# Weighing values with the values held still in TensorE and the probabilities streaming, in a local-and-global attention kernel

## The reference

```
x = x + attn(layernorm(x));  out = x + layernorm(x) @ (weight * scale[:, None]).T + bias
attn:  q, k, v = h @ Wq + bq, h @ Wk + bk, h @ Wv + bv      (split into 16 heads of 64)
  local:  each block of 128 queries sees 256 keys, from 64 before the block to 64 behind it
          ctx = softmax(q k^T / 8, outside the sequence masked) v
  global: the 62 queries with the largest norm, the first and the last see all 1024 keys;
          their rows of ctx are replaced by softmax(qg k^T / 8) v
```

## Time and profile before

| | us |
|---|---|
| median of 3 runs | 2242.92 (2241.53 to 2243.91) |
| the profiled execution's own time | 2242.39 |
| its span from first to last instruction | 2240.8 |
| TensorE busy in the span | 2166.2 (97%) |
| VectorE busy | 1486.8 (66%) |
| ScalarE busy | 827.8 (37%) |
| GpSimd busy | 596.1 (27%) |
| mean granted TensorE clock | 0.982 of full |

### The profile page before, as it was taken

The page is one execution under the profiler, slowest core; times in us unless marked ns, Lnnn a source line. Parts: engine busy times, 40 slices in busy tenths (PEclk is TensorE's granted clock), DMA queues, the critical chain, the costliest instruction groups (busy, mean ns, idle before and its releaser), DMA issues.

```text
span 2240.8 us, 38387 instructions
## 1 busy us (share of the span) xinstructions
PE 2166.2 (97%) x12768; PEld 1849.1 (83%) x12768; DVE 1486.8 (66%) x2989; ACT 827.8 (37%) x2186; POOL 596.1 (27%) x464
## 2 busy tenths in 40 slices
PE   5999999999999989999999999999999978999999
PEld 4888887888888878888888787888888877888887
DVE  6587676664876766748777666396666566666664
ACT  2334444452354444532544455325445450000000
POOL 1332232124322321243213212433132103212221
PEclk9999999999999999999999999999999978999999
DMA  3332112113322121133121211321121113333331
GB/s 141 94 97 70 61 50 78 52 31 122 96 64 67 50 77 52 31 117 99 62 70 50 77 49 34 97 80 44 52 77 43 33 50 126 140 131 125 137 140 66
DMA packets 116723, 175.35 MB, mean 78 GB/s; under 512 B 16208, under 2 KB 81814, under 8 KB 116624
## 3 DMA queue, kind: packets, MB, share of 16 engines
q1 hardware_dynamic: 108688, 155.25, 21.3%
q10 hardware_dynamic: 4608, 16.78, 1.8%
q0 software_dynamic: 3328, 2.17, 0.6%
HBM read 122.73 MB, written 51.44 MB: 78 GB/s over the span
## 4 chain that ended last, share of the span: by engine, by line
PE 87%; DVE 6%; DMA 2%; issue 2%; ACT 2%; POOL 0%; SPq 0%; DVEq 0%; POOLq 0%; ACTq 0%
PE proj L512 42%; PE proj L784 15%; PE pv L635 10%; PE turn L625 5%; PE score L610 4%; PE pv L679 3%; PE score L660 2%; DMA stat_rows<-ln_rstd 1%; PE turn L775 1%; PE misc L647 1%; PE turn L670 1%; PE turn L553 1%; DVE xT_lo L1136 1%; ACT xT_hi L825 1%; DVE top_idx L1177 0%
## 5 line engine op out<-in xcount | busy, mean ns | idle before, releaser
L512 PE MATMUL proj<-xT_hi,w_hi 128*128 128x512 f32 x1536 | 404.2, 405 | 6.5 <-DVE xT_lo L1136 5.4
L512 PE MATMUL proj<-xT_hi,w_lo 128*128 128x512 f32 x1536 | 409.7, 398 | 0.0
L512 PE MATMUL proj<-xT_lo,w_hi 128*128 128x512 f32 x1536 | 381.2, 390 | 0.0
L512 PEld LDWEIGHTS proj<-xT_lo,w_hi 128*128 128x128 f32 x1536 | 288.4, 188 | 62.4
L512 PEld LDWEIGHTS proj<-xT_hi,w_lo 128*128 128x128 f32 x1536 | 283.0, 189 | 63.2 <-issue 0.5
L512 PEld LDWEIGHTS proj<-xT_hi,w_hi 128*128 128x128 f32 x1536 | 277.3, 190 | 62.1 <-issue 6.0
L897 ACT ACTIVATE probs<-score,neg_max 128x256 f32<-128x256 f32 (+1 forms) x512 | 228.7, 459 | 184.4 <-DVE neg_max L1224 120.4
L405 POOL TENSOR_TENSOR ctx_out<-pv_sum,row_inv 128x256 f32<-128x256 f32 x128 | 84.1, 657 | 677.5 <-DVE pv_sum L1261 659.7
L381 POOL CAST w_hi<-w_raw 128x1024 fp32r<-128x1024 f32 x96 | 113.8, 1186 | 524.0 <-PE proj L512 365.3
L383 POOL TENSOR_TENSOR w_lo<-w_raw,w_hi 128x1024 fp32r<-128x1024 f32 x96 | 231.6, 2412 | 7.8
L635 PE MATMUL pv<-v_nat,pT_hi 128*128 128x128 f32 x1024 | 200.2, 278 | 15.3 <-DVE pT_lo L1240 15.3
(11 more groups left out here) (147 smaller groups left out, 3461.1 us busy)
## 6 DMA issues: line engine op xcount, KB each, us to landing
w_raw<-in_wstream SPq DMA_DIRECT2D x96, 512.0 KB, 3.9
x_buf<-in_rows SPq DMA_DIRECT2D x56, 512.0 KB, 3.3
q_rows<-q_nat SPq DMA_DIRECT2D x64, 256.0 KB, 3.0
ctx_rows<-ctx_out SPq DMA_DIRECT2D x128, 128.0 KB, 1.8
q_store<-ctx_rows SPq DMA_DIRECT2D x32, 512.0 KB, 4.2
out<-q_store ACTq DMA_DIRECT2D x32, 512.0 KB, 2.6
q_store<-in_cols SPq DMA_DIRECT2D x28, 512.0 KB, 4.0
q_store<-in_rows SPq DMA_DIRECT2D x8, 512.0 KB, 5.3
```

The costliest lines, as they stand in the source:

```text
L512: mm = pe.matmul(proj[:, bank, :], w[b][:, k * P:k * P + P], x[:, k, half * HALF:half * HALF + HALF], start=(m == 0), stop=(m == 23), skip ...
```

## The change

- **Weighing.** `weigh` holds a 128x128 piece of V still and streams probabilities. For each head of a step there are three tiles of keys. The middle one meets both blocks of queries and 64 global queries in one matmul of 320 columns, the others take 192 and 128 (192 in the last step). With high and low parts that makes 12 matmuls a step. The results lie by channel, in a new tensor `weighed` that takes the two banks of `pv` and `misc`.
- **Global queries ride along.** Of each tile of keys the probabilities of a head's 64 global queries are appended to the 128 local columns (`PIECE` = 192), so `global_weigh` goes. The global scores and exponentials move from the end of the unit to its start, and `turn_gp` is cut into four pieces, one a step, each followed by `gp_hi_out` and `gp_lo_out`. The sum of the global part is built by four `add_g` on VectorE.
- **Turning back.** ScalarE copies each step's result to `oT` (`oT_out`, 512 columns), TensorE turns it (`turn_back`, 4 transposes a step; `turn_back_g`, one a unit), and the high and low half are added as before, from the second bank of `turn`.
- **V and the global queries** are turned together at the unit's start (`turn_v` both groups, `turn_gq` with the third).
- **Order.** All orders by hand are rewritten, and so are the places of columns. `row_roots` moves from unit 3 to the end of unit 2, and SyncE writes the statistics there (`save_stats`). Reading them back stays behind unit 3's stores, now with a wait for the top search. GpSimd stores the second half's indices and gathers in unit 3 instead of 4. The load of the linear bias moves from the start to behind the attention, since its tile lends its space to `g_probs`.

```diff
             def weigh(u, s):
-                pe.wait_ge(pv_free, u * EVENTS + s + 1)
+                pe.wait_ge(weigh_free, u * STEPS + s + 1)
+                pe.wait_ge(gp_set, u * STEPS + s + 1)
+                last = s == STEPS - 1
+                spans = ((2 * s + 1, PIECE, 2 * PIECE + P, 0), (2 * s, 0, PIECE, 0),
+                         (2 * s + 2, 3 * PIECE - TOPK * last, 3 * PIECE + P, PIECE - TOPK * last))
                 for h in range(2):
+                    pe.wait_ge(pT_set, 2 * (u * STEPS + s) + h + 1)
+                    for i, (j, a, z, at) in enumerate(spans):
+                        for pt in (pT_hi, pT_lo):
+                            mm = pe.matmul(weighed[:, h, at:at + z - a], v_nat[:, j, h, :], pt[:, h, a:z],
...
+            def turn_back(u, s):
+                pe.wait_ge(oT_set, u * STEPS + s + 1)
+                if s < STEPS - 1:
+                    pe.wait_ge(pT_set, 2 * (u * STEPS + s + 1) + 2)
...
+            def turn_back_g(u):
+                pe.wait_ge(weigh_free, u * STEPS + STEPS + 1)
+                pe.wait_ge(gp_set, u * STEPS + STEPS)
+                pe.transpose(turn[:, 0:P], g_part[:, :], ident[:, :]).then_inc(g_turned, 1)
...
+            def global_scores(u, first):
+                pe.wait_ge(m_set, u * MISC + MISC)
+                pe.wait_ge(proj_free[1], first + 3)
```

More of the change, by code:

```diff
@@ L705, in attend @@
                 scores(u, 2, first)
-                part(2)
+                part(3)
+                turn_gp(u, 1)
+                turn_back(u, 0)
                 weigh(u, 1)
@@ L1027, in _ @@
         def _(dve):
-            dve.sem_inc(pv_free, 1)
+            for free in (pv_free, weigh_free, g_free):
+                dve.sem_inc(free, 1)
             dve.sem_inc(o_set, 2)
@@ L1206, in v_lo_out @@
                 dve.wait_ge(m_hi_set, u * MISC + g + 1)
+                src = weighed_banks[g] if g < 2 else turn_banks[0]
                 for rows, j, step, count, col in V_PIECES[g]:
@@ L1256, in _, with gp_lo_out @@
-            pv4 = pv[:, :].rearrange("p (g d) -> p g d", g=4)
+            def gp_lo_out(u, s):
+                dve.wait_ge(gp_hi_set, u * STEPS + s + 1)
+                count = len(step_tiles(s))
+                hi, lo = (x[:, :, :].rearrange("p h (i c) -> p i h c", c=PIECE)[:, 0:count, :, P:PIECE]
+                          for x in (pT_hi, pT_lo))
+                dve.tensor_tensor(lo, turn[:, 0:count * P].rearrange("p (i h q) -> p i h q", h=2, q=TOPK), hi.bitcast(F32),
+                                  ALU.subtract).then_inc(gp_set, 1)
@@ new lines, in add_g @@
+            def add_g(u, s):
+                dve.wait_ge(oT_set, u * STEPS + s + 1)
+                part, new = g_part[:, :].rearrange("p (h q) -> p h q", h=2), weighed[:, :, P:PIECE]
+                if s == 0:
+                    ins = dve.tensor_copy(part, new)
+                else:
+                    dve.wait_ge(weigh_free, u * STEPS + s + 1)
+                    ins = dve.tensor_tensor(part, new, part, ALU.add)
+                ins.then_inc(weigh_free, 1)
+            def inverses(u, s):
+                dve.wait_ge(exp_set, 2 * (u * STEPS + s + 1))
+                dve.wait_ge(ctx_set, u * STEPS + s + 1)
+                dve.reciprocal(row_inv[:, 4 * s:4 * s + 4], row_sum[:, 4 * s:4 * s + 4]).then_inc(inv_set, 1)
@@ L1304, in attend @@
                 columns(1)
-                v_lo_out(u, 2)
-                pv_sums(u, 0)
+                maxima(u, 1)
+                gp_lo_out(u, 0)
+                global_inverse(u)
+                add_g(u, 0)
                 p_lo_out(u, 1)
@@ L1311, in attend @@
                 columns(2)
-                pv_sums(u, 1)
+                if not last:
+                    k_lo_out(n, hp + 1, 0)
+                gp_lo_out(u, 1)
+                pv_sums(u, 0)
+                add_g(u, 1)
                 p_lo_out(u, 2)
@@ L1315, in attend @@
                 inverses(u, 2)
-                pad_q(n, u, hp, half)
                 top_norms(3)
                 columns(3)
-                pv_sums(u, 2)
-                gq_lo_out(u)
+                gp_lo_out(u, 2)
+                pv_sums(u, 1)
+                add_g(u, 2)
                 p_lo_out(u, 3)
@@ L1324, in attend @@
                 columns(4)
-                global_maxima(u)
-                if not last:
-                    k_lo_out(n, hp + 1, 0)
-                pv_sums(u, 3)
+                gp_lo_out(u, 3)
+                pv_sums(u, 2)
                 if not last:
                     split_q(u + 1, hp + 1)
-                columns(5)
-                gp_lo_out(u)
-                inverses(u, STEPS)
+                    pad_q(n, u + 1, hp + 1, (hp + 1) // HALF_PAIRS)
                 top_norms(5)
@@ L1336, in attend @@
                     row_moments(n, hp + 1)
-                if following and hp == HALF_PAIRS - 1:
+                if following and hp == HALF_PAIRS - 2:
                     row_roots(n)
-                columns(6)
+                columns(5)
+                add_g(u, 3)
                 if not last:
                     k_lo_out(n, hp + 1, 1)
+                pv_sums(u, 3)
                 g_out(n, u, hp)
```

326 lines of the change are left out of this document (173 added, 153 removed).

## The result

The changed kernel takes 2405.22 us (median of 4 runs) against 2242.23 us for the kernel before (4 runs): the ratio is 1.073, with a 95% interval from 1.071 to 1.076. The profiled execution has a span of 2402.5 us, 161.7 more than before. Forecast were 2332 us, and slower: the sign holds, but of 163 us I had counted 90, and the time lies 40 us above my own range of 2285 to 2365, inside the one I had given to the clock rival.

The account below looks back on a forecast made before the run. TensorE's own pace (42.44 us a unit) bounds the kernel, plus unit 4's waits. Saving 1.55 against 3.1 us of waits a unit, 60 us in three batches plus 30 at the end give 2332; own range 2285 to 2365, 8 in 10 2225 to 2410.

Parts of the forecast that it names:

- the clock rival: TensorE's clock falls at C in many ordinary units, 3.3 us each: 2365 to 2430 us, chance 20%.
- the third rival: Level: C and D as priced, A, B and the ends free; 2260, range 2238 to 2285 us, chance 12%.
- What TensorE saves: Matmuls and transposes gone against new ones: 1.55 us saved a unit, 48 us in 31 units.
- C: At weigh 1, TensorE waits for gp_set 1, low parts queued behind k_lo_out on VectorE: 1.65 us with restart.
- D: At weigh 2, the same wait for global probabilities without K's parts in the queue: 0.73 us with restart.
- A: At turn_p 0, a wait for V's and the global queries' low parts: 0.6 us, between 0 and 1.2.
- B: At scores 1, a wait behind the global scores' maximum and exponential: 0.1 us, between 0 and 1.
- Units 1 to 7: Batches 0 to 2: unit 2 +9.0 us, unit 3 +2.9, unit 4 -5.5, unit 5 +2.9, units 6 and 7 +5.6.
- Units 0 and 1: +3.1: First two units of batches 0 to 2: 3.1 us longer together a batch, no gather wait counted.
- The last batch and the end: Units 0 to 6 14.6 us longer, unit 7 +9, linear stage's late first load +7: together +30.
- the first rival: The same as the clock rival: the clock falls at C in many ordinary units, chance 20%.
- The second rival: The gain stands: global columns come in time, C, D, A and B vanish; near 2190, 2180 to 2238 us, 18%.

Follow-up runs that it names:

- e3: Changed kernel with turn_gp 1 and 2 ahead of parts 3 and 4, gp_hi_out ahead of the next exponentials, gp_lo_out right behind the maxima: 2319.06 us, ratio 1.036.
- e4: Changed kernel with roots put back into unit 3 and statistics stored behind unit 3's stores, as before the change: 2430.25 us, ratio 1.085.
- e5: Changed kernel with the moments of units 0 to 2 moved from ahead of add_g 3 to ahead of gp_lo_out 3: 2387.73 us, ratio 1.065.
- e1: Changed kernel with q_pad in unit 0 of each batch filled from data already in place, not the true gathered queries: 2359.06 us, ratio 1.054.
- e9: e7 with the true gathered queries of the first pair of heads, nothing left out: 2303.88 us, ratio 1.027.
- e7: e6 plus b3's split roots and e8's early loads, still without the true global queries of the first pair: 2258.64 us, ratio 1.008.
- e8: Changed kernel with the linear stage's first loads issued ahead of unit 7's last two stores and the bias: 2393.52 us, ratio 1.067.
- b3: Kernel before, roots cut in two within unit 3, statistics stored ahead of that unit's last store, unit 6's columns begun one place earlier: 2208.18 us, ratio 0.985.
- e6: Changed kernel with the edits of e1, e3 and e5 together, without the true global queries of the first pair: 2260.71 us, ratio 1.009.

## Why the prediction was right, and where it was short

**The number: right in sign, and in the outer range by its width.** 2405 us lies above my own range and in that of the clock rival (2365 to 2430), whose mechanism is seen in few units only. That it still lies under 2410 is luck: the largest piece of the 73 us that were missed, 45 us for the gather, stood in no term of the sum. The price "near 2245" in the third rival was also added up wrongly: three restarts of 3.5 us taken off 2260 leave 2249.

**What TensorE saves: right in the sum.** Twelve matmuls of the weighing were forecast at 1.46 us and take 1.42 and 1.45; four transposes 0.44. How the sum splits was not met so well: in the second head of a step, over the 122 weighings at the higher clock, the next matmul starts on average 173 ns behind the start of one of 320 columns (forecast 147), 101 ns behind one of 192 and 97 ns behind one of 128 (forecast 109). The errors cancel. An ordinary unit of 44.15 us, less C (1.52 and 0.25 of restart), D (0.60 and 0.25) and A (0.52 and 0.13, the first turns 1.03 against 0.90), leaves 40.9 us, 1.55 under 42.44.

**C, D, A, B and the ordinary unit: right.** Forecast 1.65 with restart, 0.73, 0.6 and 0.1; measured 1.77, 0.85, 0.65 and nothing in most units. 44.0 forecast, 44.15 measured in units 1 and 2 of the last batch. e3 shows it from the other side: without C and D a unit lasts 41.93. Units 4 and 5 had 45.14, 1 us more, as C and D grew to 1.88 and 1.27 there.

**Units 1 to 7: right in kind, 12 us short.** The gap in unit 2 was forecast at 3.9 us and is 5.57, the unit longer by 9.0, measured 8.8, 7.2 and 8.8. Unit 3 was forecast 2.9 us longer and is 7.3, 4.1 and 7.3. The wait for the statistics went and unit 4 fell by 5.2 us, forecast 5.5; e4 shows that it would have been 12 longer with the new form had the roots stayed. Units 6 and 7 were forecast at 48.4 and 44.5 and take 49.5 and 45.5. Units 1 to 7 of the first three batches together: 61.9 us, forecast about 50. About half of the difference is `add_g` 3 in unit 1: I said that without the roots it comes "just in time" behind the moments, and TensorE idles 1.61 us for it in units 0 and 1, so unit 1 is 3.1, 3.1 and 4.7 us longer, forecast 1.55; e5 takes that wait away. The rest is for the most part the clock in units 2 and 3 of batches 0 and 2, which together took 16.1 us more each, forecast 11.9, against 11.3 in batch 1.

**"Units 0 and 1: +3.1": the step that failed, the wait of `pad_q` taken as nothing.** The four starts of a batch, with the first unit 0, were to cost 12 us by my terms and cost 72. I had costed the move of `pad_q` by its own 0.36 us on VectorE, which was right, and had not asked what it waits for at the new place. The diff moves it past nothing but the first half of unit 0, and there the gather ends. The rows were in the trace of before: the last gather is issued at 167.27, its rows are there some 2.45 us later (by the trace after, 166.85 to 169.30), and the first maxima run at 159.18, so whatever waits for the one and stands ahead of the other costs their distance, 10.5 us. The runs give 46 us for it by e1 and 45 by e9 against e7. Of the other 14 us in these stretches `add_g` 3 and the later global columns are parts (e5, and e3's unit 0), but I did not take them apart.

**The last batch and the end: right.** +20.5 and +7.5 against about 22 and 7. The wait for `x_norm` doubled as the load went out behind the bias; e8 returned it.

**The rivals.** In ordinary units the clock at C did not fall: behind C, part 4's twelve projections take 2.94 us as before the change, and the granted clock over that unit is 1.00 (the last line below). A unit now has 68 transposes by the count of the program and idles in their midst, and keeps its clock. But the first rival is not wrong everywhere: of the 31 waits at `weigh` 1, four had the 1.2 GHz level behind them, namely unit 3 of batches 0 and 2 (2.80 us idle), unit 5 of batch 1 (1.89 us) and unit 0 of the last batch (1.52 us). The 6.1 us behind the same wait of 2.80 us in unit 3 of batches 0 and 1 (start:end, us, busy us of PE, PEld, DVE, ACT and POOL with their instructions, PEclk, DMA share, GB/s):

```profile
339.10:345.20 6.10, 6.09 (x32) 5.69 (x32) 1.91 (x4) 1.76 (x3) 3.49 (x6) 0.50 0.09 22
827.70:833.80 6.10, 6.09 (x44) 5.38 (x45) 3.10 (x9) 2.92 (x10) 3.48 (x6) 1.00 0.11 22
```

Unit 3 lasts 49.73 us in the one and 46.53 in the other, so such a fall costs 3.2 us, near the 3.3 that I had priced; the one in unit 5 cost 1.0. The clock also fell behind three of the six waits of 1.6 us for `add_g` 3, 1.6 us each time. Why behind these and not behind the others, the runs don't show. The rule of the Trainium skill, "TensorE: Matmul & The Clock Gate", Part 4 (PE-mode transpose), that I set against the change would have given the first rival's time; the ordinary units of this trace, at 1.00 with 68 transposes, don't bear it out. Nor does my reading of the earlier trace rows hold, that turns, weighing and scores alone don't bring the clock back: in b3's last unit, with nothing else on TensorE, the granted clock is 0.51 from 1789.9 to 1793.4 and 1.00 from there to 1803.6. The lower mean, 0.964, comes from stretches with long waits. Of two more stretches after, in the same form, the first holds the wait for `q_pad`, the second the ordinary unit shown above.

```profile
148.00:196.00 48.00, 33.91 (x203) 27.93 (x201) 26.33 (x54) 16.41 (x46) 14.64 (x14) 0.86 0.09 28
...
1728.00:1773.00 45.00, 42.37 (x279) 35.76 (x279) 30.12 (x62) 22.62 (x67) 10.53 (x8) 1.00 0.14 47
```

The second rival, that the gain stands, needed the global columns in time; by e3 and e6 this form can have that, at 41.9 to 42.3 us a unit, but not in the order that was given.

**What stays open:** how `pad_q` of unit 0 is to be had without the wait; the 4.05 us gap at the end of unit 6 in the new form, which no run mended; when a short wait brings the clock down; and whether the form can beat the kernel before with true queries.

## What to carry to other kernels

When an instruction moves in a hand-ordered queue, its price is not its duration but the latest thing it waits for, DMAs included, against the first thing that stands behind it: read both times in the trace of before. An equal share of work in another form pays only when each new link has a long piece behind which it can hide, so place the link first and then count the matmuls. And test the parts of a change one by one: here one of the smallest, storing statistics earlier, gave about 30 us once its block was cut in two and the columns behind it were spread.

## What the runs showed of the hardware

- From its start to the next start a matmul of 192 columns takes about what one of 128 takes, 101 and 97 ns, and one of 320 columns 173 ns; twelve of them take 1.42 to 1.45 us. The estimates of 109 and 147 ns hold for the sum only.
- Behind a wait of 0.6 or 1.5 us the same twelve take 1.67 us at a granted clock of 1.00, 0.25 more in both cases. Behind 12.63 us eight projections take 3.31 us against 1.83, at a granted clock of 0.50 up to 174.6. Behind 2.80 us, in unit 3, the clock was 0.50 in two batches and 1.00 in one, and the unit 49.7 or 46.5 us.
- Two operations of 64x64 on VectorE, 0.36 us before, took 2.22 us after, at 169.30, while GpSimd was splitting weights (168.93, 2.34 us); in the earlier trace rows three `column_lo` take 5.36 us, while GpSimd casts and splits weights (455.49 to 459.77). In these rows a small operation beside GpSimd's large ones is not small; no run takes the two apart.
- In e3 the idle time at the weighing fell by 77 us and 15 us of new waits came up; the time fell by 86. Together the waits cost more than their idle time, here by over a third, of which the higher clock of the last unit is a part.
